# Layer 3 moved into the search's stream, the opening into layer 0's, and the two streams woven by a table

## The chip, the cores and the metric

One core of a Trainium2 chip runs one program. Its engines are TensorE (PE), VectorE (DVE), ScalarE (ACT), GpSimd (POOL) and SyncE (SP, which only issues transfers); each takes its instructions strictly in the order in which they were written, and engines wait for each other by semaphores. The metric is device time in microseconds (us) from launch to end, the median of several runs.

## The reference, cut to what matters

The input has 8 items of 512 tokens and 128 channels. Each goes through four layers, and each layer multiplies an attention-like branch with a gate and adds the product to the stream:

```python
x = L0_attn_x
xn = _layernorm(x); s = _L0_attn_ref(xn, ...); g = _silu(_L0_ffn_ref(xn, ...)); x = x + s * g
xn = _layernorm(x); s = _L1_attn_ref(xn, ...); g = _silu(_L1_ffn_ref(xn, ...)); x = x + s * g
xn = _layernorm(x); s = _L2_attn_ref(xn, ...); g = _silu(_L2_ffn_ref(xn, ...)); x = x + s * g
xn = _layernorm(x); s = _L3_attn_ref(xn, ...); g = _silu(_L3_ffn_ref(xn, ...)); x = x + s * g
```

Layer 0 is a gated recurrence over time and a "coupling" network (three cycles through a four-step MLP). Layer 1 has a time mix and two blocks of local attention with a feed-forward part. Layer 2 has a state-space scan with 16 states and a mixture of four experts. Layer 3 has the same coupling network with other weights, a linear attention `o_l`, and an attention that keeps the largest weights of each row:

```python
def _L3_attn_ref(x, ...):
    ...
    aw = jax.nn.softmax(scores, axis=-1)
    kth = jax.lax.top_k(aw, topk)[0][..., -1:]
    aws = aw * (aw >= kth)
    o_s = jnp.einsum('bhnm,bhmd->bhnd', aws / (aws.sum(-1, keepdims=True) + 1e-08), v)
    ...
    return (a * o_s + (1.0 - a) * o_l) ... @ Wproj.T + bproj
```

`topk` is 25 of 512, for 16 heads and 512 rows of each item.

## The kernel before, in words

All activations stand as 128 channels by 512 tokens. The program has a setup, a block called here the separate opening, and then nine blocks with a barrier and a clearing of all semaphores between them: `run(0)` computes layers for item 0 alone, seven rounds of a loop compute the layers of one item while the search of the item before runs, and `run(B)` has the last search alone. A last block stores the result.

**The search** is what keeps the largest weights (`b_pe`, `b_act`, `b_dve`, `b_pool`). It goes over 32 pairs of head and row block. For each pair PE makes the scores, ACT copies them to `top`, DVE takes eight maxima at a time (MAX8, line 2042, eight instructions a pair) and strikes them out (MATCH_REPLACE8, line 2046, six a pair), POOL makes the mask and multiplies (lines 2105 and 2111), ACT takes the exponential (line 1980), PE transposes (line 1910) and multiplies by the values. An item has 256 MAX8 and 192 MATCH_REPLACE8.

**The streams.** Each engine's program in a block is made by two Python generators: stream a (the layers: `a_pe` and so on, which chain `l0_*`, `l1_*`, `l2_*`, `l3_*`) and stream b (the search). `weave` steps through a; at each `yield` it may step b, and what b writes until its own next `yield` stands there in the engine's queue. Each `yield` of a names a kind, and the table `ROOM` says how many steps of b a place of this kind is worth (1.8 for a "hop", 0.1 for a state of the scan): shares add up, and b is stepped at each whole one. So b never gets more than two steps at one place. All four engines use the same rule, so that a step of the search stands at the same place in each. A block has 221 steps of a and 243 of b; a pair of the search is seven steps of b.

**The stages of a.** Layer 0 (`l0_*`, to line 808), layer 1 twice (projections; attention, `L1073` to `L1084`; feed-forward, to lines 1261 and 1266), layer 2 (its start; the mixture of experts, "moe", lines 1460 to 1577; the scan over states, lines 1503 to 1625) and layer 3 (`Layer3`, `l3_*`: norm, its own attention's preparation, the coupling network). Layer 3 is followed in the same stream by the **opening** (`Opening`, lines 566 to 660): norm and projections of the next item's `x0`, needed by layer 0. For the first item the separate opening does this.

**What goes between the blocks.** Layer 3's results for the search stand in the upper part of `arena` (`vt_n`, `ol_n`, `th_n`, `kf_n`, `q_t`). At the head of the next block ACT copies `kf` and makes four masked copies `qm` (lines 1989, 1991), and POOL copies `vt`, `ol`, `th_b` and `x_b` (lines 2113 to 2116).

**Tables of ACT.** Its functions stand in sets (LN with exp, exp with tanh, GELU, SILU), and `table(name)` writes an ACT_TABLE_LOAD (line 317) when the wanted set isn't the last one. It stands mostly behind the wait for the data that the function takes.

## Time and profile before

| | us |
|---|---|
| median of 3 runs | 5811.5 (5808.37 to 5865.23) |
| the profiled execution, its own time | 5860.48 |
| its span, first to last instruction | 5858.7 |

| engine | busy us | share of the span |
|---|---|---|
| PE | 4234.7 | 72% |
| DVE | 3994.7 | 68% |
| ACT | 3039.3 | 52% |
| POOL | 2527.5 | 43% |

The mean granted clock of TensorE is 0.767 of full speed. Reading: busy time is the time in which an engine executes; no engine is busy throughout, so the time is set by chains from engine to engine, and by the engine that is busiest in each stage. Transfers are small: 44.07 MB in the whole span.

### The profile page before, as it was taken

The page shows a single profiled execution, that of the slowest core. Times are in us where ns is not written, and L with a number is a line of the kernel's source. Part 1 is how long each engine was busy: PE and PEld are TensorE (multiplying, and loading weights), DVE is VectorE, ACT ScalarE, POOL GpSimd, SP SyncE. Part 2 cuts the span into 40 slices and gives each one's busy share as a digit, 9 for nine tenths or more (in the row PEclk, how much of TensorE's full clock was granted, in tenths as well). Part 3 has the DMA queues.
Part 4 walks back from the last instruction along what each step waited for, and adds up shares of the span by engine and source line. Part 5 has one row for each costly group of instructions (what it writes and reads, how often), then busy time and mean ns, then how long its engine had stood idle before and what let it go on. Part 6 is the DMA issues. An engine that isn't in the chain of part 4 may idle for free. (4 is left out here: it accounts for less than half of the span.)

```text
span 5858.7 us, 58221 instructions
## 1 busy us (share of the span) xinstructions
PE 4234.7 (72%) x16676; PEld 1933.8 (33%) x16676; DVE 3994.7 (68%) x7874; ACT 3039.3 (52%) x5809; POOL 2527.5 (43%) x2356
## 2 busy tenths in 40 slices
PE   5776777767777677766777677776777767777676
PEld 1331234323342234422343223432244322332233
DVE  3325567776677766776667857678566786677798
ACT  3434455555555555545554555555555554565543
POOL 1103244454445344453443534436344363444466
PEclk8885788778886888858778678876787768887655
DMA  1000000000000000000000000000000000000000
GB/s 72 1 22 0 4 1 22 1 1 5 1 22 0 3 3 1 22 0 3 3 1 22 0 3 3 22 1 0 5 1 22 1 0 5 1 22 1 2 1 3
DMA packets 7995, 44.07 MB, mean 8 GB/s; under 512 B 848, under 2 KB 848, under 8 KB 7248
## 3 DMA queue, kind: packets, MB, share of 16 engines
q1 hardware_dynamic: 7632, 39.89, 1.8%
q8 instruction: 148, 2.42, 0.2%
q14 instruction: 215, 1.76, 0.1%
HBM read 37.52 MB, written 2.36 MB: 7 GB/s over the span
## 5 line engine op out<-in xcount | busy, mean ns | idle before, releaser
L2105 POOL TENSOR_SCALAR top<-top,m 128x512 f32<-128x512 f32 x512 | 808.1, 1578 | 1255.3 <-DVE m L2042 1171.5
L2042 DVE MAX8 m<-top 128x8 f32<-128x512 f32 x2048 | 1292.9, 679 | 8.3 <-ACT top L1972 7.6
L2046 DVE MATCH_REPLACE8 top<-m,top 128x512 f32<-128x512 f32 x1536 | 1026.0, 675 | 0.2
L296 PE MATMUL bank<-arena,weights 128*128 128x512 f32 (+7 forms) x1200 | 689.5, 688 | 286.8 <-ACT arena L510 56.6
L296 PE MATMUL bank<-arena,consts 128*128 128x512 f32 (+1 forms) x966 | 713.6, 835 | 72.9 <-POOL arena L1643 23.6
L2111 POOL TENSOR_TENSOR top<-top 128x512 f32<-128x512 f32 x512 | 661.6, 1292 | 24.5 <-ACT top L1980 6.5
L1910 PE MATMUL bank<-consts,top 128*128 128x128 f32 x2048 | 420.7, 342 | 247.2 <-POOL top L2111 192.5
L296 PE MATMUL bank<-arena 128*64 128x128 f32 (+4 forms) x3328 | 502.9, 370 | 119.9 <-ACT arena L1084 61.7
L1987 ACT ACTIVATE top<-bank 128x512 f32<-128x512 f32 x512 | 304.9, 596 | 473.8 <-PE bank L1910 473.3
L317 ACT ACT_TABLE_LOAD x358 | 459.3, 1283 | 110.3 <-PE bank L296 102.0
L1910 PEld LDWEIGHTS bank<-consts,top 128*128 128x128 f32 x2048 | 302.5, 175 | 569.6 <-POOL top L2111 341.3
L296 PEld LDWEIGHTS bank<-arena,weights 128*128 128x128 f32 (+4 forms) x1200 | 212.9, 205 | 672.8 <-issue 209.9
L296 PE MATMUL bank<-hold,weights 128*128 128x512 f32 (+2 forms) x520 | 306.7, 715 | 173.4 <-issue 53.9
L1972 ACT ACTIVATE top<-bank 128x512 f32<-128x512 f32 x512 | 301.7, 591 | 200.5 <-PE bank L296 144.8
L1643 POOL TENSOR_TENSOR arena<-arena 128x1024 f32<-128x1024 f32 x128 | 286.4, 2238 | 275.6 <-DVE arena L1611 274.4
L296 PEld LDWEIGHTS bank<-arena 128*64 128x64 f32 (+2 forms) x3328 | 302.8, 183 | 304.4 <-issue 215.0
L296 PE MATMUL bank<-top,vt 128*9 128x128 f32 x4096 | 365.2, 337 | 32.7 <-ACT top L1987 32.7
L296 PE MATMUL bank<-kf,qm 32*128 32x512 f32 x1024 | 370.3, 803 | 8.9 <-ACT qm L1991 6.4
L1296 POOL TENSOR_TENSOR arena<-arena 128x384 f32<-128x384 f32 (+1 forms) x256 | 197.4, 773 | 408.5 <-DVE arena L1202 408.5
L1980 ACT ACTIVATE top<-top,nmx 128x512 f32<-128x512 f32 x512 | 364.8, 716 | 1.7
L296 PEld LDWEIGHTS bank<-arena,consts 128*128 128x128 f32 (+1 forms) x966 | 213.5, 249 | 341.7 <-issue 155.3
L296 PE MATMUL bank<-l_parts,pick 96*128 96x512 bf16 x256 | 158.4, 619 | 227.2 <-DVE arena L1604 211.6
(261 smaller groups left out, 6377.0 us busy)
## 6 DMA issues: line engine op xcount, KB each, us to landing
arena<-experts_dram SPq DMA_DIRECT2D x32, 768.0 KB, 6.6
weights<-weights_dram SPq DMA_DIRECT2D x1, 6982.0 KB, 19.6
hold<-x_dram SPq DMA_DIRECT2D x9, 256.0 KB, 2.7
out_dram<-x_out SPq DMA_DIRECT2D x9, 256.0 KB, 3.5
consts<-consts_dram SPq DMA_DIRECT2D x1, 1759.5 KB, 23.3
rot<-consts_dram SPq DMA_DIRECT2D x1, 1024.0 KB, 25.3
```

Source lines behind the costliest of these rows:

```text
L296: return nc.tensor.matmul(o, lhsT, rhs, start=start, stop=stop)
L317: nc.scalar.preload_act_table_set(name)
L1296: nc.gpsimd.tensor_tensor(p, p, L.rec[f][:, 2 * e:2 * e + 2, None].to_broadcast([128, 2, KW - n0]), ALU.mult).then_inc(S["shared"], 1)
L1643: nc.gpsimd.tensor_tensor(L.hc[n % 2], L.hh[n % 2], L.cn[n % 3][:, None, :].to_broadcast([128, 2, T]), ALU.mult).then_inc(S["hc"], 1)
L1910: i = nc.tensor.transpose(Y[:, 128 * k:128 * k + 128], pp[e][:, 128 * k:128 * k + 128], C("ident"))
L1972: act(sc[slot(p, e)], X[e], ACT.Copy).then_inc(SB["sc"], 1)
L1980: act(ex[e], sc[slot(p, e)], ACT.Exp, scale=SC, bias=nmx[:, slot(p, e):slot(p, e) + 1], accum_out=zs[:, q, heads[e]:heads[e] + 1]).then_in ...
L1987: act(pt_[e], Y, ACT.Copy).then_inc(SB["pt"], 1)
L2042: nc.vector.max(m8[:, slot(p, e), k], src).then_inc(SB["top"], 1)
L2046: nc.vector.match_replace(wk_[e], m8[:, slot(p, e), k], sc[slot(p, e)] if k == 0 else wk_[e], -3e38).then_inc(SB["rest"], 1)
L2105: nc.gpsimd.tensor_scalar(pp[e], sc[slot(p, e)], m8[:, slot(p, e), TOPK // 8, 0:1], None, ALU.is_ge).then_inc(SB["kept"], 1)
L2111: nc.gpsimd.tensor_tensor(pp[e], pp[e], ex[e], ALU.mult).then_inc(SB["pp"], 1)
```

## The change

- Stream a ends with layer 2. Layer 3 stands at the head of stream b, ahead of the search of the same item, so it runs in the block in which the next item's layers run. `run(B)` now has layer 3 and the search of the last item.
- The opening stands at the head of layer 0 in stream a. The separate opening is gone, and with it one of nine openings; `x0` of the first item is loaded in the setup.
- Layer 3 works in `top` and in the PSUM banks of the search (`X`, `Y`, `P`), writes `vt`, `ol`, `kf`, `qm` and `th_b` in place, and takes its norm into `oo`. The copies at the block's head are gone, but for `x_b`. The search's first instructions on DVE and POOL wait for layer 3's last one (`gate`).
- `ROOM` gives way to `SEARCH`, a table with one digit for each step of a (base 36, `a` is ten): so many steps of b. Stream a has 200 steps, b 264. One place has ten steps of b, eight have six or five, 72 have none; 69 steps are beyond the second at their place.
- `table()` stands ahead of the wait for the data, and a tanh takes whichever of three sets is loaded.
- SP waits for `x0` ahead of the experts' transfers; each clearing has 29 rows on each engine where it had 23.

```diff
-ROOM = {"hop": 1.8, "l0": 1.0, "pj": 0.8, "at0": 0.8, "at1": 0.8, "at2": 0.7, "wo": 1.5, "ffn": 1.3,
-        "moe": 1.5, "state": 0.1, "states": 0.1, "busy": 0.3}
+SEARCH = ("0030001012121031111222010302030140211310211202111220023121011011011112100401413120420311233210122111"
...
 def weave(a, b):
-    room = 0.0
-    for kind in a or ():
-        room += ROOM[kind]
-        while b is not None and room >= 1.0:
-            room -= 1.0
+    for n, _ in enumerate(a or ()):
+        for _ in range(int(SEARCH[n], 36) if b is not None and n < len(SEARCH) else 0):
             next(b, None)
...
-        def table(name):
-            if now[0] != name:
+        def table(name, *also):
+            if now[0] != name and now[0] not in also:
...
                 for k in range(3):
+                    table(GELU)
                     a.wait_ge(*S("cn1", k + 1))
-                    table(GELU)
                     act(self.h1, b, ACT.Gelu, bias=W(lay + "_cn_b1")).then_inc(S["cn1_gelu"], 1)
...
+            yield from L.op.pe(pe)
             cp = L.cp.pe(pe)
+            pe.wait_ge(*S("op_kn", 1))
+            pe.wait_ge(*S("op_qn", 1))
             mm(A[1], W("l0_Wv"), xn0).then_inc(S["v"], 1)
...
             def __init__(L):
-                L.carve = Carve(0, EDGE)
+                L.carve = Carve(0, 14 * T, top)
...
+                for r in range(4):
+                    act(qm[:, r], F[0], ACT.Identity, scale=keep[:, 0, r:r + 1], bias=keep[:, 2, r:r + 1]).then_inc(S["mask"], 1)
...
-            act(kf[:], kf_n, ACT.Copy).then_inc(SB["mask"], 1)
-            for r in range(4):
-                act(qm[:, r], q_t, ACT.Identity, scale=keep[:, 0, r:r + 1], bias=keep[:, 2, r:r + 1]).then_inc(SB["mask"], 1)
+            yield from l3_act(a)
...
+                    if p == 0:
+                        v.wait_ge(*S3("gate", 1))
                     v.wait_ge(*SB("sc", 2 * p + e + 1))
...
-            nc.gpsimd.tensor_copy(vt[:], vt_n).then_inc(SB["taken"], 1)
-            nc.gpsimd.tensor_copy(ol[:], ol_n).then_inc(SB["taken"], 1)
-            nc.gpsimd.tensor_copy(th_b[:], th_n).then_inc(SB["taken"], 1)
-            nc.gpsimd.tensor_copy(x_b[:], x[:]).then_inc(SB["taken"], 1)
+            yield from l3_pool(g)
...
             yield from l2_dve(v)
-            yield from l3_dve(v)
```

How many of an item's 448 search instructions on DVE (MAX and MATCH_REPLACE) stand in each stage of a, counted in the written order of the loop:

| stage of a | before | after |
|---|---|---|
| (opening and) layer 0 | 50 | 20 |
| projections 0 | 36 | 44 |
| attention 0 | 44 | 58 |
| feed-forward 0, projections 1 | 52 | 74 |
| attention 1 | 44 | 62 |
| feed-forward 1, start of layer 2 | 62 | 48 |
| mixture of experts | 70 | 106 |
| scan over the states | 14 | 36 |
| layer 3 and opening | 76 | in stream b |

Three places show what moved. On DVE, in the loop, in the scan over the states of layer 2 (the second to fifth state; MAX and MATCH_REPLACE are the search's, the other two lines the scan's), before:

```order
L1604 TENSOR_TENSOR arena<-arena,bank 128x1024
L2042 MAX m<-top 128x8 x2
L1611 SCALAR_TENSOR_TENSOR arena<-bank,arena 128x512 x2
L1604 TENSOR_TENSOR arena<-arena,bank 128x1024
L1611 SCALAR_TENSOR_TENSOR arena<-bank,arena 128x512 x2
L1604 TENSOR_TENSOR arena<-arena,bank 128x1024
L1611 SCALAR_TENSOR_TENSOR arena<-bank,arena 128x512 x2
```

And the same place after:

```order
L1604 TENSOR_TENSOR arena<-arena,bank 128x1024
L2036 MAX m<-top 128x8 x2
L2040 MATCH_REPLACE top<-m,top 128x512 x2
L2036 MAX m<-top 128x8 x4
L2040 MATCH_REPLACE top<-m,top 128x512 x2
L2036 MAX m<-top 128x8 x2
L1611 SCALAR_TENSOR_TENSOR arena<-bank,arena 128x512 x2
L1604 TENSOR_TENSOR arena<-arena,bank 128x1024
L2040 MATCH_REPLACE top<-m,top 128x512 x2
L1611 SCALAR_TENSOR_TENSOR arena<-bank,arena 128x512 x2
```

Twelve instructions of the search now stand in front of one pair of the scan's own. The last eight of the 16 states have none.

On ACT, in the loop, in layer 3's coupling before (L506 to L520 are the coupling, L1768 layer 3's own softmax, L1980 the search's exponential):

```order
L506 ACTIVATE arena<-bank,weights 64x512
L1972 ACTIVATE top<-bank 128x512
L1987 ACTIVATE top<-bank 128x512
L317 ACT_TABLE_LOAD
L1980 ACTIVATE top,zs<-top,nmx 128x512 x2
L317 ACT_TABLE_LOAD
L510 ACTIVATE arena<-bank,weights 32x512
L317 ACT_TABLE_LOAD
L1768 ACTIVATE arena<-arena 128x1024
L317 ACT_TABLE_LOAD
L516 ACTIVATE arena<-bank,couple 128x512
```

After, the two couplings stand next to each other (writes to `top` are layer 3's, those to `arena` and `bank` layer 0's):

```order
L497 ACTIVATE top<-bank,weights 64x512
L759 ACTIVATE bank<-arena,consts 128x512
L488 ACTIVATE arena<-bank,couple 128x1
L501 ACTIVATE top<-bank,weights 32x512
L309 ACT_TABLE_LOAD
L1764 ACTIVATE top<-top 128x1024
L309 ACT_TABLE_LOAD
L507 ACTIVATE top<-bank,couple 128x512
L511 ACTIVATE top<-top,couple 128x512
L493 ACTIVATE arena<-bank,weights 128x512
L759 ACTIVATE bank<-arena,consts 128x512
```

Here the GELU of both layers need one set. Over one block of the loop the loads go from 47 to 38: from 22 to 12 in layers 0 and 3 and the opening, from 25 to 26 elsewhere.

## Rows read from the trace of the kernel before

**Rows 1.** Stores of the results, one at the head of each block with a search.

```profile
L2178 SPq DMA_DIRECT2D out_dram<-x_out x8: 348/351/370, 622.1 to 5548.0; - x8
```

**Rows 2.** Stretch, length, busy PE PEld DVE ACT POOL, PEclk, DMA, GB/s: three loop blocks.

```profile
2018.50:2714.30 695.80, 507.73 (x2082) 234.24 (x2082) 498.32 (x981) 380.53 (x726) 316.26 (x294) 0.80 0.02 6
2714.30:3435.10 720.80, 533.58 (x2082) 245.24 (x2082) 498.31 (x982) 380.72 (x726) 316.15 (x294) 0.76 0.02 6
4134.50:4855.10 720.60, 533.63 (x2082) 245.24 (x2082) 498.24 (x982) 380.74 (x726) 316.13 (x294) 0.76 0.02 6
```

**Rows 3.** The same by stage, first block, no search; layer 0 to opening.

```profile
57.10:121.00 63.90, 50.23 (x92) 16.82 (x92) 28.03 (x36) 24.42 (x35) 13.85 (x11) 0.85 0.00 1
121.00:171.90 50.90, 40.98 (x106) 18.21 (x106) 22.51 (x32) 22.35 (x34) 10.99 (x10) 0.81 0.02 6
171.90:222.60 50.70, 32.70 (x222) 20.67 (x222) 10.24 (x30) 25.63 (x83) 12.36 (x16) 0.76 0.00 1
222.60:289.90 67.30, 52.45 (x148) 22.26 (x148) 26.56 (x38) 26.86 (x42) 10.12 (x8) 0.92 0.00 0
289.90:339.90 50.00, 32.07 (x222) 20.32 (x222) 10.24 (x30) 25.60 (x83) 12.36 (x16) 0.76 0.00 0
339.90:392.00 52.10, 33.72 (x85) 14.84 (x86) 15.66 (x32) 19.21 (x26) 0.28 (x3) 0.78 0.16 61
392.00:452.80 60.80, 52.94 (x131) 22.60 (x130) 16.47 (x24) 19.92 (x33) 0.00 (x0) 0.89 0.00 0
452.80:533.10 80.30, 50.33 (x68) 12.99 (x67) 62.22 (x55) 31.47 (x48) 54.74 (x31) 0.50 0.00 0
533.10:596.40 63.30, 39.98 (x76) 14.98 (x76) 20.27 (x39) 25.21 (x38) 2.53 (x2) 0.63 0.00 0
596.40:618.00 21.60, 12.14 (x16) 3.95 (x16) 2.08 (x4) 11.65 (x16) 1.26 (x1) 0.66 0.00 0
```

**Rows 4.** The same stages in the last loop block, with search; then the boundary.

```profile
4855.10:4943.30 88.20, 66.97 (x168) 23.95 (x168) 58.08 (x109) 46.14 (x73) 34.93 (x35) 0.81 0.00 1
4943.30:5003.90 60.60, 50.92 (x186) 23.99 (x186) 43.03 (x84) 30.48 (x55) 27.90 (x27) 0.84 0.01 5
5003.90:5057.50 53.60, 35.89 (x302) 22.76 (x302) 36.04 (x91) 34.94 (x106) 27.32 (x32) 0.90 0.00 1
5057.50:5146.70 89.20, 68.56 (x262) 32.94 (x262) 59.62 (x121) 44.33 (x77) 34.93 (x31) 0.87 0.00 1
5146.70:5197.20 50.50, 36.61 (x298) 23.05 (x300) 39.13 (x93) 36.50 (x107) 30.83 (x37) 0.91 0.00 1
5197.20:5269.80 72.60, 52.27 (x221) 26.34 (x218) 56.53 (x127) 38.09 (x64) 28.69 (x30) 0.76 0.11 44
5269.80:5361.00 91.20, 76.79 (x279) 34.88 (x278) 62.27 (x130) 51.92 (x88) 30.35 (x30) 0.86 0.00 1
5361.00:5447.00 86.00, 54.43 (x95) 15.91 (x95) 70.55 (x76) 33.49 (x55) 60.72 (x37) 0.52 0.00 0
5447.00:5523.40 76.40, 56.13 (x224) 25.27 (x226) 67.91 (x147) 49.95 (x84) 33.63 (x32) 0.73 0.00 1
5523.40:5544.60 21.20, 12.61 (x59) 5.46 (x54) 5.23 (x11) 14.86 (x25) 6.89 (x5) 0.97 0.00 0
5544.60:5551.60 7.00, 2.08 (x4) 0.50 (x4) 0.00 (x0) 3.52 (x6) 2.38 (x4) 0.50 0.10 37
```

**Rows 5.** Busy time in the last block, search alone.

```profile
5560.00:5850.00 290.00, 195.75 (x905) 95.61 (x906) 275.38 (x642) 119.42 (x257) 192.79 (x190) 0.50 0.00 1
```

**Rows 6.** Busy time, attention 0 in the slower block of rows 2.

```profile
2871.20:2929.50 58.30, 42.30 (x302) 26.41 (x302) 35.95 (x91) 34.93 (x106) 27.32 (x32) 0.77 0.00 1
```

**Rows 7.** Groups by line, ACT, last loop block: table loads.

```profile
L317 ACT ACT_TABLE_LOAD x47 | 60.3, 1283 | 12.9 <-PE bank L296 12.2
```

**Rows 8.** In order of time: end of the setup, start of the separate opening.

```profile
31.27 0.62 DVE L390 TENSOR_SCALAR keep<-consts,by_channel 128x4 f32<-128x4 f32 x4
32.68 0.33 SPq L2216 DMA_DIRECT2D hold<-x_dram  x1
```

More of the change, by code:

```diff
@@ L320, in build @@
         LN, TANH, GELU, SILU = "natural_log_exp_and_others", "exp_and_others", "gelu_and_others", "silu_and_others"
-        def exp_table():
-            if now[0] not in (LN, TANH):
-                table(LN)
         def clear(sems):
@@ L2147, in a_pe, with a_act @@
             yield from l2_pe(pe)
-            yield from l3_pe(pe)
-        def a_act(a, first):
+        def a_act(a):
             yield from l0_act(a)
@@ L2153, in a_act @@
             yield from l2_act(a)
-            yield from l3_act(a, first)
         def a_dve(v, first):
@@ L2192, in _ @@
                 def _(a):
-                    weave(a_act(a, first) if item else None, b_act(a) if search else None)
+                    weave(a_act(a) if item else None, b_act(a) if search else None)
                 @block.vector
@@ L2200, in _ @@
                 def _(g):
-                    weave(a_pool(g, first) if item else None, b_pool(g) if search else None)
+                    weave(a_pool(g) if item else None, b_pool(g) if search else None)
             marks.settle()
```

237 lines of the change are left out of this document (107 added, 130 removed).

## The prediction

> **What bounds the kernel now.** I read the stores first, to find the blocks. They stand at 622.1 and, the eighth, at 5548.0 [rows 1]. So the span is 57.1 us of setup and separate opening, 565 us of layers alone (57.1 to 622), 4926 us for seven blocks of the loop, and 311 us of the last search (5548 to 5858.7). 84% of the time is the loop, 703.7 us a block.
>
> Then the busy time by block. One takes 695.8 us, the next 720.8 us, with the same DVE time (498.3 us) and a granted clock of 0.80 against 0.76 [rows 2]. The difference sits where the clock does: attention 0 takes 58.3 us at 0.77 [rows 6] and 53.6 us at 0.90 [rows 4], and PE's busy time times the clock is the same (42.3 × 0.77 = 32.6, 35.9 × 0.90 = 32.3). A second slower block of 720.6 us stands in [rows 2]; the other five average (4926 − 1441)/5 = 697, so the two cost 2 × 24 = 48 us. The profiled execution took 5860.5 us, 49 us over the median of 5811.5: I read the median as an execution without such blocks, and forecast one.
>
> Last, the stages with and without search. In the loop no engine is full: of 695.8 us PE has 508, DVE 498, ACT 381, POOL 316 [rows 2]. Alone the layers need 561 us, layer 0 to opening [rows 3]. The search alone is DVE: 275.4 of 290.0 us [rows 5], in which stand 250 MAX8 and 186 MATCH_REPLACE8, so 290/436 = 0.665 us for one (I call it an op). Together they take 689.5 us without the boundary [rows 4]: 128 us more than the layers alone. So two chains that wait on themselves are laid over each other, and a block gets shorter if more of the one fits into the gaps of the other. Layer 3 is the worst chain: alone it takes 63.3 us with DVE busy for 20.3 and ACT for 25.2 [rows 3].
>
> **The change, step by step (one block of the loop).**
>
> *Layer 3 and the opening leave the end of stream a:* −97.6 us (76.4 + 21.2) [rows 4], with 76 ops.
>
> *Opening, layer 0 and layer 3 together take the place of layer 0.* Layer 0 took 88.2 us with 50 ops [rows 4]. Now the a chain is 21.6 + 63.9 = 85.5 us and layer 3's is 63.3 us [rows 3], with 20 ops behind it. Below: no less than the PE's work, 12.1 + 50.2 us for a, 40.0 × 0.63/0.73 = 34.5 us for layer 3 (0.63 is its clock alone, 0.73 beside the search), and 195.75 × 20/436 × 0.50/0.85 = 5.3 us for 20 ops of the search [rows 5]: 102 us. Above: the chains one after the other, 85.5 + 63.3 + 20 × 0.665 = 162 us. Between them I go by the share of PE: the fullest stage of the trace is the mixture of experts, 76.8 of 91.2 us or 84% [rows 4]. 102/0.85 = **120 us**, that is +31.8. DVE (28.0 + 2.1 + 20.3 + 13.3 = 64 us) doesn't bound it.
>
> *106 ops more stand in layers 1 and 2* (428 for 322, by the counts beside the change). Each costs between nothing (in the gaps) and 0.665 us: 0 to 70 us. By stage, with what an op cost there so far (the stage with search less without [rows 3, 4], by its ops):
> - projections 0: 9.7/36 = 0.27; +8 ops, +2.2.
> - attention 0: 2.9/44 = 0.07; +14 ops fill DVE to 36.0 + 9.3 = 45.3 of 56 us, I take 0.2 each: +2.8.
> - feed-forward 0 and projections 1: 21.9/52 = 0.42; +22, +9.2.
> - attention 1: 0.5/44 = 0.01, but +18 ops make DVE's work 39.1 + 12.0 = 51.1 us, more than the 50.5 us of the stage. Layer 3's stage held DVE at 67.9/76.4 = 89%: 51.1/0.89 = 57.4, +6.9.
> - feed-forward 1 and start of layer 2: 20.5/62 = 0.33; −14, −4.6.
> - mixture of experts: 30.4/70 = 0.43; +36, +15.6.
> - scan: 5.7/14 = 0.41; DVE is 70.6 of 86.0 us already, and all ops stand before the ninth state, so nearly full price: 22 × 0.65 = +14.3.
>
> Sum +46.4 us: layers 1 and 2 go from 503.7 to 550.1. Their DVE share goes from 367/504 = 73% to (367 + 70)/550 = 79%.
>
> *Boundary:* 7.0 us [rows 4]; the clearing grows by 6 rows on 23, in proportion at most 1.8, I take 0.5. The copies at the block's head go, which stood beside layer 0's start: nothing. The waits that the change adds: SP's for `x0` holds only the experts' transfers, which wait for layer 1's attention anyway, some 250 us later [rows 4]. The search's first MAX waits for layer 3's `gate`; behind it on DVE is layer 0's work. If layer 3 is late, layer 0 is late with it, which is the 120 above.
>
> *Table loads:* 47 to 38 a block, 1.283 us each [rows 7]: 11.5 us of ACT, nearly all in layers 0 and 3, where I count them as part of what makes 85% reachable. Loads written ahead of a wait can use the 12.2 us a block that ACT waited for PE just before one [rows 7]; I take that as mostly off the path, 0 of 12. The Trainium skill, ScalarE: Activation LUTs, section What ACT_TABLE_LOAD costs, adds a drain of about 1380 ns to each switch. By that nine loads would be worth 24 us and not 11.5. The trace doesn't agree: 60.3 us for 47 loads is the load alone, and the sum goes by it.
>
> Block: 120 + 550.1 + 7.5 = **677.6 us**, against 696 before.
>
> **The rest.** Setup to the first block: the setup's last work ends at 31.9, the separate opening's transfer went out at 32.7 [rows 8]; the block starts near 33.5. Opening 21.6, layers 0 to 2 476.0 (57.1 to 533.1) [rows 3], end of block 4 (618 to 622): 535, less some 4 for loads ahead of their waits: 531. Last block 63.3 + 310.7 = 374, less 1 for the copies. Sum 904, where before 57.1 + 565 + 311 = 933 stood: one opening of 21.6 us, its barrier and its transfer are gone. Total: 904 + 7 × 677.6 + 1.8 (time outside the span) = **5649**, rounded to 5650 us, 2.8% under the median. The same sum for before, 933 + 7 × 697 + 1.8, gives 5814.
>
> **Rivals.**
>
> *1. The bunches are paid in full.* `weave` before never put more than two steps of the search at one place. Now 69 of 264 steps are beyond the second at their place, ten at one. An engine works in order, so behind a bunch layer 2's next matmul or scan row waits, and what follows on the other engines. A step is 9.3/7 = 1.33 us (14 ops a pair). 69 × 1.33 = 92 us in place of the 46.4: a block of 723, 5968 us in all, slower by 2.7%. For it: the expert stage double-buffers only two pieces of 60.8/17 = 3.6 us [rows 3]. Against: each engine is at another place of the same table at a time, so one is in the bunch while others are past it, and 71 places have none. It decides from 65 us on (block 696); at 77 us it is slower by 1%.
>
> *2. The two coupling chains add.* They stand alternately on PE, ACT, DVE and POOL, so each step of one may wait for the other's: 162 us for 120, block 720, 5943 us, slower by 2.3%. For it: PE is busy for 50 of 63.9 us in layer 0 already. Against: the search's 50 ops cost layer 0 only 24 us, and each chain is mostly an engine waiting for another. The gain is gone at 138 us.
>
> *3. TensorE's clock rises.* Layer 3 alone has 0.63, the opening 0.66, the scan 0.50, the search alone 0.50 [rows 3, 5], while layer 3 with search has 0.73 and its opening 0.97 [rows 4]. If the first stage went to 1.0, PE's work there would be 8 + 43 + 25 + 5 = 81 us, 95 at 85%, block 653, 5475 us. The Trainium skill, TensorE: Matmul & The Clock Gate, section What's actually happening, says that activity releases a clock that is low by default; that speaks for this rival, and the rise from 0.63 to 0.73 with the search agrees. Against: layer 0 stayed at 0.81 with the search (0.85 without), and the scan at 0.52.
>
> *4. Less cover than before:* ops at their full price (70) and 128 us for the first stage, block 709: 5870 us. With one of the two, 697 to 702: no change.
>
> **Chances.** Forecast (block 655 to 692) 0.70; clock 0.08; bunches 0.11, of which half ends within 1%; chains add 0.06; rival 4 0.05, within 1%. A measurement of this kernel can tell about 1% from no change. So faster 0.78, same 0.12, slower 0.10. The range is from a block of 656 to one of 700: 5497 and 5805, rounded to 5500 and 5800; the forecast's own is 5490 to 5750. An execution with blocks at the lower clock is 24 us longer for each.
>
> **What would show it.** In the profile of the changed kernel: blocks of about 678 us; from the block's start to line 806 (layer 0's last) 120 us, PE at 85%; layers 1 and 2 in 550 us with DVE at 79%; attention 1 at 57; mixture of experts at 107; scan at 100; 38 table loads a block. PE waiting over 5 us behind a search row in the expert stage or in the scan's first half would speak for rival 1, a first stage over 138 us for rival 2, a clock near 1.0 in it for rival 3. I am wrong if a block takes over 692 us.

## The result

The changed kernel takes 5397.2 us (median, 5384.2 to 5400.2) beside 5835.5 us (5808.4 to 5865.2) for the one before: a ratio of 0.924 (0.918 to 0.930). The forecast was 5650 us, 5500 to 5800. So the sign was right and the gain over twice as large as forecast. The profiled execution took 5400.2 us, 1.9 us more than its span. From its page: the span and busy times, the stores (source lines have moved from L2178 to L2166), and the table loads.

```profile
span 5398.3 us, 58321 instructions
PE 4091.9 (76%) x16660; PEld 1894.8 (35%) x16660; DVE 4012.1 (74%) x7871; ACT 2922.0 (54%) x5717; POOL 2520.7 (47%) x2324
L309 ACT ACT_TABLE_LOAD x294 | 377.2, 1283 | 5.2
```

The stores, with first and last start:

```profile
L2166 SPq DMA_DIRECT2D out_dram<-x_out x8: 349/350/369, 529.8 to 5023.1; - x8
```

A loop block by stage (the last), cut as in [rows 4]: first stage (opening, layer 0, layer 3), projections 0, attention 0, feed-forward 0, projections 1, attention 1, feed-forward 1, start of layer 2, experts, scan, boundary, and the whole block:

```profile
3753.00:3862.30 109.30, 91.62 (x200) 32.82 (x200) 63.13 (x108) 68.03 (x104) 25.58 (x23) 0.84 0.00 1
3862.30:3920.70 58.40, 52.48 (x191) 24.13 (x191) 48.60 (x98) 33.18 (x61) 29.92 (x28) 0.82 0.02 5
3920.70:3974.40 53.70, 39.35 (x330) 24.65 (x330) 43.65 (x105) 37.51 (x112) 33.39 (x38) 0.94 0.00 1
3974.40:4007.20 32.80, 26.60 (x134) 12.64 (x134) 29.75 (x68) 18.40 (x35) 16.26 (x16) 0.95 0.00 1
4007.20:4062.80 55.60, 46.79 (x188) 22.71 (x186) 47.20 (x92) 29.93 (x58) 29.68 (x27) 0.91 0.00 0
4062.80:4118.90 56.10, 42.63 (x314) 27.68 (x314) 41.25 (x103) 36.83 (x111) 34.02 (x40) 0.82 0.01 1
4118.90:4157.10 38.20, 28.68 (x134) 12.87 (x134) 34.01 (x72) 22.98 (x41) 19.48 (x19) 0.91 0.22 83
4157.10:4180.70 23.60, 17.56 (x67) 9.70 (x68) 21.33 (x53) 18.45 (x30) 6.13 (x8) 0.72 0.00 0
4180.70:4280.20 99.50, 85.50 (x355) 39.48 (x354) 83.24 (x178) 57.56 (x100) 48.46 (x48) 0.88 0.00 1
4280.20:4379.40 99.20, 60.85 (x174) 23.17 (x173) 89.26 (x114) 42.38 (x73) 72.53 (x47) 0.64 0.00 0
4379.40:4388.00 8.60, 0.04 (x1) 0.04 (x1) 0.02 (x1) 0.00 (x0) 0.61 (x1) 0.67 0.13 39
3753.00:4388.00 635.00, 492.11 (x2083) 229.90 (x2083) 501.45 (x981) 365.24 (x715) 316.05 (x291) 0.83 0.02 7
1166.20:1814.70 648.50, 504.96 (x2083) 235.12 (x2083) 500.75 (x981) 365.17 (x715) 315.49 (x290) 0.81 0.02 7
1334.00:1395.00 61.00, 46.97 (x340) 28.76 (x342) 42.61 (x105) 36.80 (x110) 34.36 (x39) 0.78 0.00 1
```

The seven blocks take (5023.1 − 529.8)/7 = 641.9 us each, where the forecast had 677.6. What lies around them is 529.8 + (5398.3 − 5023.1) = 905 us, forecast 904. So the whole miss is in the loop: 35.7 us a block, 250 us in seven. The last two rows are another block and its attention 0: again, as in [rows 2, 6], the same program has blocks at a lower clock (648.5 us at 0.81), here 13 us longer. Of these, 7.3 us stand in attention 0 (0.78 instead of 0.94), and 7.0 us in feed-forward 1 with the start of layer 2 (68.8 us at 0.75 instead of 61.8 at 0.84).

In the table an "op" is, as in the prediction, one MAX8 or MATCH_REPLACE8 of the search.

| stage | ops before, after | us before | forecast | us after |
|---|---|---|---|---|
| opening, layers 0 and 3 | 126, 20 | 185.8 | 120 | 108.7 to 110.2 |
| projections 0 | 36, 44 | 60.6 | 62.8 | 57 to 59 |
| attention 0 | 44, 58 | 53.6 | 56.4 | 54 to 61 |
| feed-forward 0, projections 1 | 52, 74 | 89.2 | 98.4 | 88.4 |
| attention 1 | 44, 62 | 50.5 | 57.4 | 55 to 56 |
| feed-forward 1, start of layer 2 | 62, 48 | 72.6 | 68.0 | 62 to 69 |
| experts | 70, 106 | 91.2 | 106.8 | 99.4 |
| scan | 14, 36 | 86.0 | 100.3 | 99.9 |
| boundary | | 7.0 | 7.5 | 8.1 |

Layers 1 and 2 average 524 us (641.9 − 109.4 − 8.1), forecast 550.1; in the last block DVE is busy for 85% of them (438 of 517 us), forecast 79%. Of the 35.7 us a block, 26 are missing here and 11 in the first stage.

Which wait could be the price of the bunches? In the experts and in the scan of the last block (the view of waits: us in all, times, longest):

```profile
ACT arena L1459 <- PE bank L288: 20.7, 10, 3.3
PE bank L288 <- DVE arena L1604: 24.1, 14, 3.7
POOL arena L1642 <- DVE arena L1611: 15.3, 10, 7.6
```

The experts' SILU (L1459) waits at most 3.3 us for its matmul, and PE in the scan at most 3.7 us for a DVE row that may stand behind a bunch. Only POOL's product over the states once waits longer, 7.6 us.

### The profile page after: what moved, and what is told of

The parts are those of the page before. It is cut to its first block and busy times, and to the rows that moved or that the text cites. A ratio compares the mean times of both kernels' runs of the same rounds, so it can differ in the third digit from the quotient of the medians.

```text
span 5398.3 us, 58321 instructions
## 1 busy us (share of the span) xinstructions
PE 4091.9 (76%) x16660; PEld 1894.8 (35%) x16660; DVE 4012.1 (74%) x7871; ACT 2922.0 (54%) x5717; POOL 2520.7 (47%) x2324
## 5 line engine op out<-in xcount | busy, mean ns | idle before, releaser
L288 PE MATMUL bank<-arena,consts 128*128 128x512 f32 (+1 forms) x912 | 624.7, 779 | 114.8 <-ACT arena L406 42.3
L288 PE MATMUL bank<-arena,weights 128*128 128x512 f32 (+8 forms) x976 | 536.8, 669 | 87.3 <-issue 20.7
L1901 PE MATMUL bank<-consts,top 128*128 128x128 f32 x2048 | 417.6, 340 | 192.7 <-POOL top L2108 137.6
L288 PE MATMUL bank<-arena 128*64 128x128 f32 (+3 forms) x3200 | 474.5, 371 | 44.9 <-ACT arena L1083 40.2
L1901 PEld LDWEIGHTS bank<-consts,top 128*128 128x128 f32 x2048 | 303.8, 175 | 477.7 <-POOL top L2108 282.7
L1981 ACT ACTIVATE top<-bank 128x512 f32<-128x512 f32 x512 | 305.6, 597 | 298.0 <-PE bank L1901 297.4
L288 PE MATMUL bank<-top,vt 128*9 128x128 f32 x4096 | 344.0, 323 | 141.4 <-ACT top L1981 141.4
L309 ACT ACT_TABLE_LOAD x294 | 377.2, 1283 | 5.2
L1974 ACT ACTIVATE top<-top,nmx 128x512 f32<-128x512 f32 x512 | 365.3, 721 | 0.9
L1295 POOL TENSOR_TENSOR arena<-arena 128x384 f32<-128x384 f32 (+1 forms) x256 | 197.5, 775 | 340.9 <-DVE arena L1201 340.8
L288 PEld LDWEIGHTS bank<-arena 128*64 128x64 f32 (+2 forms) x3200 | 277.4, 181 | 215.1 <-issue 166.2
L820 POOL TENSOR_TENSOR arena<-arena,hold 128x512 f32<-128x512 f32 x64 | 83.7, 1308 | 539.2 <-DVE arena L793 539.1
L288 PEld LDWEIGHTS bank<-arena,consts 128*128 128x128 f32 (+1 forms) x912 | 190.8, 235 | 363.4 <-issue 134.1
L288 PEld LDWEIGHTS bank<-arena,weights 128*128 128x128 f32 (+5 forms) x976 | 175.3, 201 | 398.8 <-issue 197.1
```

The costliest lines, as they stand in the source:

```text
L288: return nc.tensor.matmul(o, lhsT, rhs, start=start, stop=stop)
L309: nc.scalar.preload_act_table_set(name)
L1295: nc.gpsimd.tensor_tensor(p, p, L.rec[f][:, 2 * e:2 * e + 2, None].to_broadcast([128, 2, KW - n0]), ALU.mult).then_inc(S["shared"], 1)
L1901: i = nc.tensor.transpose(Y[:, 128 * k:128 * k + 128], pp[e][:, 128 * k:128 * k + 128], C("ident"))
L1974: act(ex[e], sc[slot(p, e)], ACT.Exp, scale=SC, bias=nmx[:, slot(p, e):slot(p, e) + 1], accum_out=zs[:, q, heads[e]:heads[e] + 1]).then_in ...
L1981: act(pt_[e], Y, ACT.Copy).then_inc(SB["pt"], 1)
```

## The experiments

"The table" is `SEARCH`. A pair of the search is seven steps of stream b, and what these steps hold differs: one has the scores, others the transposes on PE with the copies on ACT and the masks on POOL. I call **phase** the step of the pair that falls on a given place of the layers. The kernel before measured 5845 to 5859 us beside these runs.

### Which part of the change brings what

**The old rule on the new streams.** The table is replaced by what `ROOM` (times 1.285, so that 264 steps find room) gives.

```diff
-SEARCH = ("0030001012121031111222010302030140...
+SEARCH = ("2223223222111211211121121113223223...
```

> The changed kernel, but the search's steps are placed by the rule of before: the kinds' rates of the table ROOM, all multiplied by 1.285 so that 264 steps fit into 200 places (the opening's places count as hops). Computes the same. Theory 1 (the move of layer 3 and of the opening is what counts, where the search stands within the layers matters little): within 1% of the changed kernel's 5397 us, 5345 to 5450, blocks of 635 to 650 us. Theory 2 (the places of the table are what made the added search instructions cheap, about 0.2 us each where I had priced them at 0.44): the prices of my sum hold again, a block of about 678 us, 5650 us in all. Theory 3 (the order of the table saves table loads: 49 loads a block here, 38 there, 1.283 us each): at most 11 x 1.283 = 14 us a block, 5500 us.

5703.7 us, ratio 0.973 (0.969 to 0.977); block 686. That is −2.7%, the size that was forecast for the whole change, but by chance: its parts aren't those of the forecast. The two rows are its first stage, where the rule packs layer 3 into the first ten places and has 62 ops behind it, and its layers 1 and 2:

```profile
3960.40:4114.10 153.70, 113.81 (x284) 40.25 (x284) 88.01 (x168) 91.19 (x136) 41.96 (x40) 0.78 0.00 0
4114.10:4635.70 521.60, 396.60 (x1797) 191.92 (x1798) 409.96 (x813) 291.89 (x591) 274.23 (x250) 0.80 0.02 7
```

The first stage is 44 us longer than the changed kernel's, and that is the whole difference between the two blocks. Layers 1 and 2 have 386 ops here, 64 more than before, and take 18 us more than the 503.7 of before: 0.28 an op. So already without the table an added op was cheaper than 0.44. Theory 3 can't carry the difference either: the page counts 357 table loads, 47 a block for 38, which is 11.5 us of ACT for 44 us.

**The table's numbers, spread evenly.** Each stage keeps its number of steps; within it they stand at equal distances, so no place has more than three.

```diff
-SEARCH = ("0030001012121031111222010302030140...
+SEARCH = ("0110011012112121121121121211211211...
```

> The changed kernel, with as many search steps in each stage as its table has, but spread evenly over the places of the stage (at most three at one place, where the table has up to ten); 39 table loads a block for 38. Computes the same. Theory 1 (only the number of steps in a stage counts): 5397 us within 0.5%. Rival 1 of the prediction in part (bunches cost something, evenly spread is better): 5300 to 5370 us. Theory 2 (the exact places count, bunches stand where an engine would be idle): 5480 to 5600 us, and the longer stages are those with bunches, the mixture of experts and the scan.

5474.7 us, 0.934 (0.931 to 0.938); block 652. The experts take 100.2 us with 100 ops by the written order, where the table's bunches take 99.4 with 106, and the scan 100.0 for 99.2 to 99.9. Bunches as such cost nothing here. The exact places are worth the rest, 0.934 against 0.924: some 60 us by the ratios, 77 by the medians. Theory 2 had the size (5480) but not the stages: on the average of the seven blocks projections 0 (63.1 us for 58.3) and feed-forward 0 (36.9 for 32.8) are the longer ones, not those with bunches. Its layers 1 and 2:

```profile
3905.50:4436.50 531.00, 392.28 (x1878) 193.57 (x1878) 430.92 (x864) 295.14 (x610) 290.83 (x267) 0.84 0.02 7
```

That is more than the 521.6 us of the old rule, with 36 ops more. What this kernel gains on the old rule, it gains in the first stage (112.7 us for 153.7).

**Loads behind their waits again**, in the changed kernel, at 20 places (a 21st, at the head of the scan, stays ahead), with a tanh in one set only; still 38 a block.

```diff
-                table(GELU)
                 a.wait_ge(*S("gc1", 1))
+                table(GELU)
```

> The changed kernel with its ACT table loads written behind the waits again, as before (19 places), and tanh bound to one set; 38 loads a block as in the changed kernel. Computes the same. If loads ahead of waits matter: up to the 12.2 us a block that ACT waited ahead of loads before, 5397 + 85 = 5480 us. If they were off the path, as I took it: 5397 us within 0.5%.

5436.8 us, 0.928 (0.924 to 0.931). By the medians that is 40 us more than the changed kernel, by the ratios 20; projections 0 take 59 to 62 us for 57 to 59. PE and DVE are busy as long as in the changed kernel (4087.6 for 4091.9 us, 4017.0 for 4012.1). The page's group shows the wait that the load stood behind (in the changed kernel it reads 5.2):

```profile
L309 ACT ACT_TABLE_LOAD x294 | 377.2, 1283 | 189.6 <-PE bank L288 139.2
```

**And ahead of their waits in the kernel before**, nothing else changed (47 a block).

> The kernel before with only the loads changed: ACT table loads ahead of the waits, tanh from any of three sets; 47 loads a block as before. Computes the same. If loads ahead of waits matter: up to 12 us a block less, 5812 - 85 = 5730 us. If they are off the path: no change, 5812 to 5835 us.

5826.6 us, 0.996 (0.994 to 0.998): 20 to 25 us. So having the loads ahead of their waits is worth 3 to 6 us a block, not all of the 12.2 us of [rows 7] and not nothing.

### The first stage

**Layer 3's 22 steps packed** into the first ten places, as in new_room, with the rest of the table as it is.

```diff
-SEARCH = ("003000101212103111122201...
+SEARCH = ("222322322200000000000201...
```

> The changed kernel with layer 3's 22 steps packed into the first ten places (2 or 3 at each), where the table spreads them over 21; everything behind the 21st place as in the table, 20 search instructions in the first stage. Computes the same. If the packing matters (layer 3's chain stands in front of the opening's and layer 0's next step, rival 2 of the prediction in part): first stage 109 + 15 to 25 us, 5500 to 5570 us in all. If only the number of instructions counts: 109 us, 5397 us within 0.5%.

5585.4 us, 0.954 (0.949 to 0.959). The first stage grows by 31 us a block; layers 1 and 2 stay within what the changed kernel's own blocks show (520 to 524 us, there 517 to 532):

```profile
3208.80:3349.00 140.20, 102.25 (x200) 34.72 (x200) 62.94 (x109) 74.69 (x108) 24.43 (x22) 0.77 0.00 0
```

PE's 200 instructions are the changed kernel's, and they take 140.2 us instead of 109.3; PE waits more and runs at 0.77. ACT has two table loads more a block (308 for 294 on the page), 2.6 of the 31 us at most. That is rival 2, and it depends on the places: spread over 21 places layer 3 hides behind layer 0, in ten it doesn't.

**64 ops in the first stage**, 21 steps taken from the scan. The digits of places 21 to 32:

```diff
-201030203014
+333333433333
```

> The changed kernel with 64 search instructions on DVE in the first stage where it has 20, all behind layer 3 (its 22 steps stay at their places, 37 steps follow in the last 12 places), and with 21 steps fewer in the scan, which so has none. Computes the same. The kernel with the rule of before has 62 there and layer 3 packed into the first ten places, and takes 154 us. If the number of search instructions makes the 154 us: 150 to 157 us here too. If it was the packing of layer 3 into the first places: 109 + 44 x 0.5 = 131 us. The scan falls to 82 us in both cases.

5454.5 us (one run). First stage 134.6 us, +25.3 for 44 ops, 0.58 each: near the 131 of the packing theory. The scan without ops takes 90.1, not the expected 82: 36 ops cost 9.8 us there, 0.27 each, and another 9.8 us over the 80.3 of the layers alone [rows 3] stand there with no op at all, beside the search's other steps (13 are left in the last 34 places):

```profile
3136.10:3270.70 134.60, 106.38 (x288) 40.79 (x288) 90.56 (x172) 81.79 (x130) 42.60 (x40) 0.83 0.00 1
3686.20:3776.30 90.10, 52.58 (x98) 16.63 (x97) 68.89 (x62) 33.33 (x52) 56.08 (x32) 0.56 0.00 0
```

**No ops in the first stage**, 16 steps moved to the scan. It was meant to give the price of the 20 ops there.

```diff
-201030203014
+000000000000
```

> The changed kernel with no search instruction in the first stage (opening, layer 0, layer 3): the 16 steps that stood there behind layer 3 are spread over the scan, which gets 50 steps (68 search instructions on DVE for 36), evenly. Computes the same. First stage now 109 us with 20 instructions. If an instruction costs there what I assumed (the stage is 85% PE, the search adds its PE work): 109 - 6 = 103 us. If the first stage is where the search is dear (154 us with 62 instructions against 109 with 20, 1.06 us each): 109 - 21 = 88 us. Scan: 100 us with 36, price 0.665 each: 121 us.

5921.5 us (one run), slower than the kernel before. The first stage gave back only 3.2 us (0.16 an op), but all later stages got slower with the same digits and nearly the same number of ops: projections 1 63.0 us for 55.6, attention 1 65.0 for 55.9, experts 112.3 to 115.5 for 99.4. I had not expected that: the search now stood 16 steps, two pairs and two steps, behind at every place.

**The scan's steps one by one**, 34 on 34 places, in place of bunches of six and five:

```diff
-0060100330151000002000101010002520
+1111111111111111111111111111111111
```

(The last 34 places; the table's own text ends one digit earlier, and a missing digit counts as 0.)

> The changed kernel with the 34 steps of the scan spread evenly, one at a place, where the table has bunches of 6, 3, 3, 5 in the first half and 5 near the end. Computes the same. The kernel with evenly spread steps in all stages had 42 search instructions in the scan and 100.0 us, the changed kernel 36 and 99.9 us. If even is better there: 36 instructions cost 36/42 of the 20 us over 80, 97 us, 20 us less in all, 5377 us. If the bunches are no worse: 5397 us.

5380.4 us (5354.4 to 5392.8), 0.919 (0.915 to 0.923); scan 100.5 to 100.9 us. Its difference to the changed kernel is less than a measurement can tell. The bunches that the forecast pointed at (twelve of the search's instructions in front of one pair of the scan's own) cost nothing.

### The phase

**Fourteen steps** (two pairs exactly) moved from the first stage to the scan's last half, all other digits as in the table. Of places 21 to 32 only the first keeps its two steps:

```diff
-201030203014
+200000000000
```

> The changed kernel with 14 steps of the search (two pairs of seven) taken from the first stage and put into the last half of the scan; first_none had moved 16. All other digits of the table stay. Theory 1 (phase: the table's places fit one position of the seven-step pair, and 14 is a whole number of pairs): layers 1 and 2 up to the scan go back to the times of the changed kernel, attention 1 at 55 to 56 us, mixture of experts at 99 to 101, feed-forward 0 plus projections 1 at 88 to 90; only the scan is longer (64 of the search's instructions in place of 36, 108 to 118 us), the first stage 105 to 108; block 645 to 655, 5430 to 5490 us. Theory 2 (the search being late as such slows the later stages, by its data or by its buffers): as first_none, attention 1 at 63 to 65, experts at 110 to 113, block 705 to 720, 5840 to 5940 us.

5523.9 us (one run). Attention 1, experts, scan:

```profile
3474.30:3530.70 56.40, 41.42 (x310) 26.33 (x310) 41.33 (x103) 35.83 (x109) 34.03 (x40) 0.82 0.00 1
3597.70:3699.50 101.80, 84.55 (x356) 39.08 (x354) 82.81 (x179) 57.89 (x101) 48.38 (x48) 0.89 0.00 1
3699.50:3820.00 120.50, 74.45 (x230) 29.94 (x229) 104.43 (x154) 48.54 (x89) 84.25 (x59) 0.60 0.00 0
```

The layers' stages are back at the changed kernel's times although the search is fourteen steps late (attention 1 56.4 us, experts 101.8, where 99.4 stood). Only the scan is clearly longer, by 20.6 us for 28 ops, 0.74 each.

**Two steps** moved in the same way:

```diff
-201030203014
+201030203012
```

> The changed kernel with 2 steps of the search taken from the end of the first stage and put into the last half of the scan. All other digits of the table stay, so every place behind the first stage gets the search's work two steps earlier in its pair. Theory 1 (phase): the same shift as first_none's 16 steps (two pairs and two), so the later stages slow as there: attention 1 near 65 us, experts near 112, block 700 to 715, 5800 to 5900 us. Theory 2 (being late by 16 steps is what cost first_none its time): two steps cost an eighth of that, block 642 to 652, 5400 to 5470 us.

5878.7 us, 1.003 (1.001 to 1.006), block 710: two of 264 steps, and the whole gain is gone. Attention 1 and experts:

```profile
3707.00:3772.40 65.40, 46.58 (x310) 27.93 (x308) 42.76 (x105) 36.08 (x110) 35.79 (x40) 0.73 0.00 1
3847.00:3957.80 110.80, 85.96 (x355) 39.45 (x354) 83.37 (x178) 61.86 (x106) 45.17 (x45) 0.88 0.00 1
```

In the experts PE and DVE are busy as long as in the changed kernel (86.0 for 85.5, 83.4 for 83.2), ACT 4 us longer, and the stage is 11.3 us longer at the same clock of 0.88: most of that is waiting. Table loads don't explain it: the pages of the two count 308 and 294, two more a block or 2.6 us, where the block is 68 us longer.

**Four steps** (the last digit becomes zero).

> As phase_2 with 4 steps moved. Theory 1 (phase): any shift that is not a multiple of seven loses the fit; block 680 to 720, 5670 to 5920 us, with the losses in other stages than at a shift of two. Theory 2 (lateness): block 645 to 660, 5420 to 5520 us. If 4 steps cost nothing and 2 do, it is one place of the table at one phase and no general fit.

5966.6 us (one run), block 720 to 727, here with the experts at 123 and attention 1 at 63 to 66. Lateness as a cause has fallen: 14 steps cost only what the scan pays, 2 and 4 cost 480 and 570 us. (phase_4 has five table loads a block more, 6.4 of its 81 us.)

**Two steps, with the evenly spread table**, whose last two digits of the first stage go from 2 and 1 to 1 and 0.

> new_even (the table's number of steps for each stage, spread evenly within it) with the same two steps moved from the first stage to the scan. Theory 1, if the fit lies in the exact places: an evenly spread table has at most one or two steps per place and has no fit to lose, so the time stays at 5475, 5450 to 5510 us, block 650 to 657. Theory 3: the stages react to the phase whatever the spread (a step with transposes meets a chain at a bad place): 5600 to 5900 us, block 672 to 715.

5741.1 us, 0.980 (0.975 to 0.985): 266 us slower than new_even. So sensitivity isn't a matter of bunches. (Two more table loads a block, 2.6 of 38 us.) Attention 1 has 62 ops by the written order in both and took 54.8 us in new_even, 76.2 here, the widest gap of any stage. The waits of new_even in that stage, and then of this kernel:

```profile
ACT arena L1083 <- PE bank L925: 11.5, 10, 2.0
DVE arena L1201 <- ACT arena L1072: 9.7, 13, 1.2
POOL arena L1295 <- DVE arena L1201: 8.0, 15, 1.9
```

```profile
POOL arena L1295 <- DVE arena L1201: 38.4, 15, 6.3
ACT arena L1083 <- PE bank L925: 24.5, 9, 6.6
DVE arena L1201 <- ACT arena L1072: 16.7, 14, 2.0
```

They are attention's own ring: exponentials (L1072), their sums' reciprocals (L1201), the division (L1295), the transposes (L925), their copy (L1083). A few rows in order of time show the meeting (start, length, engine, line; in brackets the idle time before and its releaser):

```profile
3652.64 0.66 PE L1901 MATMUL bank<-consts,top 128*128 128x128 f32 x4 [2.07 <-POOL top L2108]
3653.33 0.60 ACT L1981 ACTIVATE top<-bank 128x512 f32<-128x512 f32 x1 [1.41 <-PE bank L1901]
3653.82 0.71 ACT L1974 ACTIVATE top<-top,nmx 128x512 f32<-128x512 f32 x1
3654.53 0.71 ACT L1974 ACTIVATE top<-top,nmx 128x512 f32<-128x512 f32 x1
3655.23 0.58 ACT L1083 ACTIVATE arena<-bank 128x512 f32<-128x512 f32 x1
3655.87 1.98 PE L288 MATMUL bank<-arena 128*64 128x128 f32 x16 [2.14 <-ACT arena L1083]
3656.83 0.17 DVE L1201 RECIPROCAL arena<-arena 128x2 f32<-128x2 f32 x1 [1.72 <-ACT arena L1072]
3657.07 0.83 POOL L1295 TENSOR_TENSOR arena<-arena 128x384 f32<-128x384 f32 x1 [4.49 <-DVE arena L1201]
3659.59 2.08 PE L288 MATMUL bank<-kf,qm 32*128 32x512 f32 x4
```

PE stands at the search's transposes (L1901) for POOL's product. Then the layer's copy on ACT (L1083) comes late, behind the search's copy (L1981) and two exponentials (L1974), PE idles again, and so POOL's division has waited 4.5 us. And after these pauses the matmuls are slow: the last two PE rows ran at a granted clock of 0.50, the first at 1.00. In new_even, at the phase that fits, the same work:

```profile
3488.47 1.13 PE L288 MATMUL bank<-kf,qm 32*128 32x512 f32 x4
3490.87 1.09 PE L288 MATMUL bank<-arena 128*64 128x128 f32 x16 [0.69 <-ACT arena L1083]
```

1.13 against 2.08 us and 1.09 against 1.98: these two rows of new_even ran at 1.00, so the pairs show the clock's two levels (2.4 and 1.2 GHz). Over the stage PE's busy time grows from 41.3 us at 0.94 to 52.3 at 0.70 for nearly the same work (38.8 and 36.6 when multiplied by the clock):

```profile
3463.00:3517.80 54.80, 41.26 (x342) 26.00 (x338) 44.51 (x114) 39.90 (x117) 35.06 (x40) 0.94 0.01 1
```

```profile
3621.00:3697.20 76.20, 52.30 (x322) 31.36 (x320) 48.22 (x119) 40.60 (x119) 36.77 (x41) 0.70 0.00 1
```

How much of the 21 us is the waits and how much the slow matmuls, which lengthen the ring and so the waits, these runs don't separate.

**Five steps, evenly spread**, from the last four places of the first stage.

> new_even with five steps moved from the first stage into the scan. If the evenly spread table is good only at its own phase (the numbers of steps for each stage carry the fit): 5600 to 5900 us, block 670 to 715, as phase_2_even. If the shift of two was an unlucky one: 5450 to 5560 us.

5647.5 us, 0.966 (0.962 to 0.970); block 669 to 679, attention 1 62 to 72. So of the three phases measured new_even is best at its own, and the numbers of steps for each stage carry part of the fit.

**The same shift under the old rule**, in the new structure and, by two and four steps, in the kernel before. In the latter:

```diff
+            if n >= 20 and late:
+                late -= 1
+            else:
+                next(b, None)
+        if b is not None and n in (180, 188):
+            next(b, None)
```

> new_room (the changed kernel's streams under the old rule, 5704 us) with two steps moved from the first stage into the scan. Theory A: the block moves from 686 us by 10 to 40 us in either direction, with attention 1 off its 55 us by over 4; 5420 to 5990 us. Theory B: within 5 us a block, 5670 to 5740 us.

> The kernel before with its rule, but two steps of the search taken from the end of layer 0 and put into the scan's last half, so the search stands two steps earlier in its pair at every place of layers 1 and 2. Theory A (the old rule stood at no special phase, and its stages vary with the phase as those of the new kernel do): the loop's block moves by 5 to 30 us in either direction, 5600 to 6050 us in all. Theory B (only a table fitted to one phase is sensitive; the old rule is near the mean at any phase): block within 5 us, 5800 to 5870 us.

> As old_phase_2 with four steps. Theory A: another value in 5600 to 6050 us, differing from old_phase_2 by over 50 us. Theory B: 5800 to 5880 us.

room_phase_2 takes 5652.6 us, 0.965 (0.961 to 0.969), 51 us under new_room. old_phase_2 takes 5783.3, 0.987 (0.984 to 0.991), old_phase_4 5804.4, 0.991 (0.988 to 0.995). In old_phase_2 attention 0 goes from 53.6 to 61.1 us and feed-forward 0 with projections 1 from 89.2 to 83.1. So under the old rule the stages vary as well, but partly cancel. Theory A holds in direction, with a smaller swing than it gave: room_phase_2 moved by 7 us a block where A had 10 to 40 and B at most 5, and the two old phases differ by 21 us where A had over 50. The phases measured so far, us:

| steps set by | phases measured | span of them | mean |
|---|---|---|---|
| old rule, old streams | 5852, 5783, 5804 | 69 | 5813 |
| old rule, new streams | 5704, 5653 | 51 | 5678 |
| even, table's numbers | 5475, 5741, 5647 | 266 | 5621 |
| the table | 5397, 5879, 5967 | 570 | |

### The price at the margin

**Seven steps out of the place with ten**, a whole pair, so no later phase changes; one by one into the scan's last half, or into the first stage behind layer 3.

```diff
-...26030a2025106024101...
+...2603032025106024101...
```

> The changed kernel with seven steps (one pair, fourteen of the search's instructions on DVE) taken out of the place that has ten in the mixture of experts and put one by one into the scan's last half. At the average of the fitted table (0.36 us an instruction in this stage, 38.6 us over the layers alone for 106) the expert stage goes from 99.4 to 94.4; if the bunch is paid in full (rival 1 of the forecast: a step 1.33 us) to 90.1; if it costs nothing, 98 to 100. The scan goes from 99.9 to 110 at phase_14's 0.74 an instruction. Block 642 to 650, 5400 to 5460 us.

> The same seven steps put into the first stage, one by one behind layer 3. The first stage goes from 109 us to 111.4 at the 0.17 that its first twenty instructions cost, to 117 at first_62's 0.58. Everything between, a whole pair later, keeps its time within 2 us (attention 1 55 to 57, feed-forward 0 32.8, projections 1 55.6); the experts at 90 to 99 as in moe_seven_less. Block 636 to 650, 5350 to 5460 us. A faster kernel than the changed one if the experts give more than the first stage takes.

moe_seven_less: 5412.7 us, 0.924 (0.917 to 0.932). Its experts and scan, and the experts of a block of moe_to_first:

```profile
3528.80:3615.80 87.00, 73.56 (x327) 34.23 (x326) 74.12 (x158) 53.68 (x92) 42.50 (x42) 0.99 0.00 1
3615.80:3729.80 114.00, 68.04 (x201) 25.88 (x201) 98.61 (x134) 45.05 (x81) 79.57 (x54) 0.62 0.00 0
3525.80:3615.90 90.10, 78.94 (x327) 36.01 (x326) 74.31 (x159) 54.01 (x93) 42.42 (x42) 0.92 0.00 1
```

The experts give 12.5 us back for 14 ops, 0.89 each, and the scan takes 14.1, 1.0 each. In the experts PE's work (busy time by clock) fell only from 75.2 to 72.8; its clock went from 0.88 to 0.99, and at 0.88 those 72.8 would be 82.7 us of PE for the 73.6 measured. So 9 of the 11.9 us that PE's busy time fell are the clock. Not all of that reaches the stage: in moe_to_first the same instructions took 86.7 us in blocks at 0.99 (PE busy for 73.5) and 90.0 to 90.4 at 0.92 (the row's 78.9): 3.4 us of the stage for 5.4 us of PE. By that share the clock is worth some 6 of the 12.5 us, an estimate. None of the three theories had so much: 87.0 us lies even under the 90.1 at which a bunch is paid in full, 1.8 us a step. That doesn't bring rival 1 back, since the bunches spread out (new_even) cost as much as the bunches; it shows that the last pair in this full stage is dear, and not that a bunch is.

moe_to_first: 5373.8 us (5366.5 to 5386.3), 0.919 (0.912 to 0.925); first stage 116 to 121 (0.7 an op), experts 86.6 to 90.4. It is the fastest kernel of the study, by 0.4%, which is less than a measurement can tell; the table is near a balance.

## Why the prediction was wrong

**Fixed part, 904 us: right** (905), and with it the argument on the separate opening. **Boundary:** 8.1 for 7.5. **Scan: the number was right, by luck**, 99.9 for 100.3. DVE is nearly full there (89.3 of 99.2 us), but the ops weren't at nearly full price: all 36 cost 9.8 us, 0.27 each, and as much again stood there without any op (first_62), which the sum had no term for.

**First stage, 120 us: the PE-work term was mis-sized.** The share was right: 91.6 of 109.3 us, 84%, forecast 85%. The work was 102 us in the sum and 91.6 in the trace. Multiplied by the clock it is 77 us of work where the sum had 81. The rest is the clock: the sum took it from the stages as they were (0.73 for layer 3), and it came out at 0.84 to 0.86. So rival 3 came in by about a quarter (from 0.79 to 0.84, of 1.0), where I had weighed it as all or nothing. The Trainium skill, TensorE: Matmul & The Clock Gate, section What's actually happening, says that activity releases the clock; the trace agrees only in part. Together the chains run at 0.84 to 0.86, above the 0.74 that opening, layer 0 and layer 3 alone average by PE's busy time (0.66, 0.85 and 0.63 in [rows 3]). But layer 0 alone had 0.85 already, and the changed kernel's first block, opening and layer 0 without layer 3, has 0.91:

```profile
33.50:113.20 79.70, 59.13 (x108) 19.52 (x108) 30.53 (x40) 35.58 (x50) 13.89 (x11) 0.91 0.00 0
```

**106 more ops, +46.4 us: the step that failed.** Layers 1 and 2 grew by 21 us, 0.2 an op, and not by 0.44. Three stages hold most of the 26 us between: feed-forward 0 with projections 1 (88.4 for 98.4), the experts (99.4 for 106.8) and projections 0 (58.3 for 62.8). I priced each stage by what its ops had cost on average under the old rule. That price is one of a phase and of places that nobody had chosen; the changed kernel's are fitted, and there the average over all ops is lower too: all 428 cost 112 us (524 less the 412 of [rows 3]), 0.26 each, before 0.28. Where the fit is gone, two steps off, layers 1 and 2 take 591.7 us (709.6 − 109.6 − 8.3), 0.42 an op in all. The evenly spread table, over three phases, took 531, 574 and 560 us there, mean 555. That this is near my 550 is no support for the sum: these are three phases of seven, and by stage the errors cancel (on average experts 98.4 us for 106.8, attention 1 65.5 for 57.4).

Nor is the fit the whole of it. Under the old rule on the new streams 64 added ops cost 0.28 each (521.6 us; in room_phase_2's block 514.3, 0.17 each). At 0.28, 106 ops would be 30 us and not 46, an estimate that takes the price as even. How much of the 26 us is the fit of the places and how much a price that was too high at any places, these runs don't separate.

And no single price would have done. One measured by moving steps was 0.16 us an op for the first 20 in the first stage and 0.58 for the next 44; 0.27 for the first 36 in the scan, then 0.74 and 1.0; and 0.6 to 0.9 for the last pair in the experts, where a pair more also went with a lower clock (0.88 for 0.92 to 0.99). The dearest lie above the 0.665 that I had as the upper bound.

**Table loads, "0 of 12 us":** measured 20 to 40 us in all, 3 to 6 a block. Count (38 a block) and length (1283 ns) were right.

**Rival 1, bunches paid in full:** fell. Spread out, the scan took 100.5 to 100.9 us for 99.9 and the experts 100.2 for 99.4. **Rival 2, the chains add:** false at the table's places, true where layer 3 is packed (140 us, over the 138 that I had given as the point of decision). **Rival 4:** fell, first stage and layers 1 and 2 were both shorter than forecast. (Of the chances, those of the rivals add up to 0.105 for the same and 0.115 for slower, where 0.12 and 0.10 were written; nothing hangs on it.)

**The range** was too narrow because it held no case in which the table is worth something in itself. From the views of the kernel before nothing gives its size. But two of them hinted at it: a table of 200 digits in place of 12 rates can hold a fit, and the seven-step pair meets layers with their own period, so a price by stage had to depend on where the pair stands. A case "the places fit", worth some 25 us a block, would have reached 5475, still over the 5397 measured.

So of the 7.6%: 2.7 came with the streams alone under the old rule, 3.9 more with the numbers of steps for each stage and with layer 3 spread over its places, and 1.0 more with the exact places; 0.3 to 0.7 of the whole is the loads ahead of their waits. More than the whole of the 3.9 stands in the first stage (41 us a block, while layers 1 and 2 grew by 9): packing layer 3 costs 19 us there beside 62 to 64 ops (153.7 and 134.6) and 31 beside 20, and the ops moved out give the rest. This part holds at every phase measured (first stage 109.6 us in phase_2, 110.7 in phase_2_even, 111.2 in even_phase_5). What holds at one phase only is that layers 1 and 2 stay at 524 to 531 us: elsewhere they take some 550 to 610, more than the 514 to 522 under the old rule, and the gain shrinks or goes. Not shown: which digits carry the fit, why the table's and not another phase suits attention 1, and what the four phases not run would give.

## What to carry to other kernels

When two streams are woven step by step, what a step costs can depend on which step meets which place as much as on how many there are. Here an edit that shifted one stream by two to five steps changed most stages behind it, and the whole time by about 1% under the old rule and by 3 to 11% with the table or its numbers, and such a shift can hide or fake the effect of the edit itself. Compare variants at the same phase (shift by whole periods), take a price from a pair moved without a shift and not from the average of a stage, and tune the table last, since here a shift by two steps undid it.

## What the runs showed of the hardware

- The clock can multiply a change in waiting. The same attention stage, with the same number of ops, ran at 0.94 (54.8 us) and at 0.70 (76.2 us). Behind two pauses of about 2 us each a group of four matmuls ran at 0.50 and took 2.08 us; without such pauses it ran at 1.00 and took 1.13. But waiting alone can do it too: phase_2's experts are 11.3 us longer at an unchanged 0.88.
- The experts with one pair less ran at 0.99 instead of 0.88. In moe_to_first the same instructions of that stage took 86.7 us at 0.99 and 90.0 to 90.4 us at 0.92, in blocks of one execution.
- Identical blocks of one execution differ by 13 us (635.0 and 648.5), with the clock in attention 0 (53.7 us at 0.94, 61.0 at 0.78) and in feed-forward 1 with the start of layer 2 (61.8 us at 0.84, 68.8 at 0.75).
- An ACT_TABLE_LOAD written ahead of a semaphore wait overlaps the wait: the idle time before the loads fell from 189.6 to 5.2 us, and of that 20 to 40 us came off the time.
